# Third gating cycle of a Trainium2 transformer block: regrouped, second layer in three passes, gates finished on ScalarE

## What is computed

```python
def _twist(x):
    o_r, o_i, p_r, p_i = jnp.split(x, 4, axis=-1)
    return jnp.concatenate([p_r, -p_i, -o_r, o_i], axis=-1)
...
gf = _global_net(x.mean(axis=1, keepdims=True), ...)
out = x
for _ in range(NUM_CYCLES):                    # 3
    tf = _coupling_net(out, ...)               # 512 -> 512 -> 256 -> 128 -> 1, gelu, sigmoid
    combined = 0.7 * gf + 0.3 * tf
    coupling = BASE_COUPLING + adaptive_range * (combined - 0.5) * 2.0
    out = out + coupling * _twist(out)
return out
```

## Time and profile before

| | us |
|---|---|
| median of 3 runs | 1733.85 |
| lowest and highest | 1733.26, 1734.9 |
| the profiled execution | 1734.33 |
| its span, first to last instruction | 1732.5 |
| feed-forward part within the span | from about 1243.4 to the end |

### The profile page before, as it was taken

The page is one execution under the profiler, slowest core; times in us unless marked ns, Lnnn a source line. Parts: engine busy times, 40 slices in busy tenths (PEclk is TensorE's granted clock), DMA queues, the critical chain, the costliest instruction groups (busy, mean ns, idle before and its releaser), DMA issues. The chain is left out here.

```text
span 1732.5 us, 34074 instructions
## 1 busy us (share of the span) xinstructions
PE 1703.2 (98%) x12392; PEld 1282.1 (74%) x12392; DVE 1443.0 (83%) x2554; ACT 1237.3 (71%) x2169; POOL 660.4 (38%) x590
## 2 busy tenths in 40 slices
PE   8999999999999999999999999999999999999997
PEld 7888888777777777777777777777775675774873
DVE  6554545999999999999999999999678976968868
ACT  4222224999999999999999999999664374365454
POOL 3432342423278552587432875543235010100100
PEclk9999999999999999999999999999999999999999
DMA  7777675765468665567764676555503514222101
GB/s 279 274 246 284 234 268 153 190 183 135 138 162 191 132 150 123 136 212 142 160 152 118 183 172 134 136 110 152 165 11 93 168 50 122 89 74 49 64 1 49
DMA packets 160951, 254.70 MB, mean 147 GB/s; under 512 B 25488, under 2 KB 77968, under 8 KB 160800
## 3 DMA queue, kind: packets, MB, share of 16 engines
q1 hardware_dynamic: 110416, 158.84, 29.1%
q0 software_dynamic: 49808, 92.82, 23.8%
q10 hardware_dynamic: 576, 1.05, 0.2%
HBM read 168.47 MB, written 84.18 MB: 146 GB/s over the span
## 5 line engine op out<-in xcount | busy, mean ns | idle before, releaser
L1021 DVE CUSTOM_DVE_ANT_0 a_neg<-a_sc_ps,am 128x1024 f32<-128x1024 f32 x512 | 622.0, 1215 | 1.4 <-PE a_sc_ps L853 1.3
L961 ACT ACTIVATE a_prob<-a_neg,a_row_min 128x1024 f32<-128x1024 f32 x512 | 586.2, 1145 | 13.5 <-DVE a_row_min L1021 7.8
L867 PEld LDWEIGHTS a_tr_ps<-ident,a_prob 128*128 128x128 f32 x4096 | 461.2, 140 | 89.3 <-issue 53.4
L867 PE MATMUL a_tr_ps<-ident,a_prob 128*128 128x128 f32 x4096 | 519.8, 274 | 0.9 <-ACT a_probT L939 0.9
L996 DVE COPY a_probT<-a_tr_ps 128x512 f32<-128x512 f32 x512 | 350.7, 685 | 37.4 <-PE a_tr_ps L867 36.0
L939 ACT ACTIVATE a_probT<-a_tr_ps 128x512 f32<-128x512 f32 x512 | 304.4, 595 | 35.4 <-PE a_tr_ps L867 15.9
L749 POOL DMA_DIRECT2D a_q_st<-q_parts x144 | 79.6, 558 | 195.6 <-PE a_sc_ps L853 159.7
L853 PE MATMUL a_sc_ps<-k_first,a_q_st 96*128 96x512 f32 x384 | 126.5, 427 | 0.1
L853 PE MATMUL a_sc_ps<-a_k_st,a_q_st 96*128 96x512 f32 x384 | 126.2, 427 | 0.0
L887 PE MATMUL a_o_ps<-a_probT,a_v 128*32 128x256 f32 x2048 | 123.6, 382 | 0.6 <-ACT a_o L950 0.6
L887 PE MATMUL a_o_ps<-a_probT,v_first 128*32 128x256 f32 x2048 | 123.8, 382 | 0.0
(11 more groups left out here) (223 smaller groups left out, 3140.8 us busy)
## 6 DMA issues: line engine op xcount, KB each, us to landing
a_q_st<-q_parts POOLq DMA_DIRECT2D x144, 128.0 KB, 3.8
k_first<-k_parts POOLq DMA_DIRECT2D x24, 512.0 KB, 7.9
a_k_st<-k_parts POOLq DMA_DIRECT2D x24, 512.0 KB, 8.3
a_m_raw<-mask SPq DMA_DIRECT2D x24, 512.0 KB, 5.2
a_adj_raw<-adj SPq DMA_DIRECT2D x24, 512.0 KB, 6.2
k_parts<-p_out_hi SPq DMA_DIRECT2D x32, 256.0 KB, 4.4
k_parts<-p_out_lo SPq DMA_DIRECT2D x32, 256.0 KB, 6.6
v_all<-p_v_out SPq DMA_DIRECT2D x8, 1024.0 KB, 4.4
```

Source lines behind the costliest of these rows:

```text
L867: last = pe.transpose(tr_ps[:, bank(u, half), j * P:(j + 1) * P], prob[:, r % NPROB, t * P:(t + 1) * P], ident[:])
L961: act.activation(prob[:, r % NPROB, :], neg[:, r % 2, :], ACT.Exp, scale=-1.0, bias=row_min[:, r % 2:r % 2 + 1], accum_out=row_sum[:, r // ...
L1021: dve.tensor_tensor_reduce(out=neg[:, r % 2, :], in0=sc_ps[:, r % 2, :], in1=am[:, 2 * qb + qt, :], scale=-1.0, scalar=3.4e38, op0=ALU.add ...
```

## The change

`SPLIT` becomes the pair of cycles (0, 2): the second layer of the first and the third cycle is done in three passes. As w2_hi and w2_lo are overwritten by the next attention tile before the third cycle, POOL copies them (`keep_w2`) to the place of pair_hi and pair_lo, which are free after the first layer. In batch 0 this stands ahead of POOL's last `split_weighted`. Gelu tiles of the second cycle, and the rounded ones of the third, lie where the second half's attention tiles X1 are; so that half's load is now released by the last second layer of the batch, and comes behind the first half's.

The third cycle is regrouped: u = (beta B + A) + c1 (B - beta A), with beta = c0 and the value in brackets kept from the second cycle. VectorE computes B - beta A (`turned`) while the second gate is still being computed, in pieces placed between the mixes, and then scales and adds (`third_cycle`). ScalarE does the affine step of the gate that VectorE did (`gate`: tanh, then an Identity with scale and bias). The rows that SP carries are beta and c1, and VectorE forms the two coefficients from the columns (`gated_columns`). On ScalarE most gelus of the next cycle's tiles now stand ahead of the gate. Two result tiles of the first half have their twisted part made by ScalarE.

```diff
@@ -1045,7 +1045,7 @@
     CYCLES = 3
-    SPLIT = 1
+    SPLIT = (0, 2)
...
@@ -1072,8 +1072,11 @@
         w2_lo = nc.alloc_sbuf_tensor_at("f_w2_lo", [P, ET, F2], F32R, offset=SB_K0 + 12288)
+        w2_kept = [nc.alloc_sbuf_tensor_at(f"f_w2_kept{part}", [P, ET, F2], F32R, offset=sb.offset + 4096 * part) for part in range(2)]
         pair_hi = sb("f_pair_hi", [P, 2, CH], F32R)
         pair_lo = sb("f_pair_lo", [P, 2, CH], F32R)
+        h1_second = [nc.alloc_sbuf_tensor_at(f"f_h1_second{j}", [P, ET, CH], F32, offset=SB_AM + 8192 * j) for j in range(NJ)]
+        u_hi_third = [nc.alloc_sbuf_tensor_at(f"f_u_hi_third{j}", [P, ET, CH], F32R, offset=SB_AM + 8192 * j) for j in range(NJ)]
...
@@ -1255,12 +1255,18 @@
         def _(pool):
+            def keep_w2(b):
+                pool.wait_ge(product_ready, 4 * ET * NJ * (b + 1))
+                pool.wait_ge(w2_lo_ready, b + 1)
+                for kept, tile in zip(w2_kept, (w2_hi, w2_lo)):
+                    pool.dma_start(kept[:], tile[:]).then_inc(w2_kept_loaded, 16)
             def load_attention(b, j, part):
                 if j == 0:
-                    pool.wait_ge(z2_ready, 2 * turn(b - 1, SPLIT - 1, 1) + 2)
+                    pool.wait_ge(z2_ready, 2 * turn(b - 1, 0, 1) + 2)
+                    pool.wait_ge(w2_kept_loaded, 32 * b)
                 else:
-                    pool.wait_ge(product_ready, 4 * ET * (NJ * (b - 1) + j + 1))
+                    pool.wait_ge(z2_ready, 2 * turn(b - 1, CYCLES - 1, 1) + 2)
...
@@ -1292,10 +1298,13 @@
                 if first:
-                    for n in range(LATE, 2 * B * GPB):
+                    for n in range(LATE, 2 * B * GPB - 1):
                         split_weighted(pool, weighted, n)
+                keep_w2(b)
+                if first:
+                    split_weighted(pool, weighted, 2 * B * GPB - 1)
                 if more:
-                    for j in (1, 0):
+                    for j in range(NJ):
...
@@ -1373,20 +1382,24 @@
                         pe.wait_ge(shared_read, 4 * ET * NJ * (b + 1))
+                if n in SPLIT:
+                    pe.wait_ge(w2_lo_ready, b + 1)
+                    if n:
+                        pe.wait_ge(w2_kept_loaded, 32 * (b + 1))
+                w_hi, w_lo = w2_kept if n else (w2_hi, w2_lo)
+                high = u_hi_third[j] if n else u_hi[j]
                 for t in tiles:
...
+                    if n in SPLIT:
                         pe.wait_ge(u_lo_ready, ET * turn_split(b, n, j) + t + 1)
...
+                    else:
+                        pe.wait_ge(h1_ready, ET * k + t + 1)
+                    for m in range(2):
+                        ms = slice(m * P, (m + 1) * P)
+                        if n in SPLIT:
+                            last = three_pass(pe, acc[:, 2 * j + m, :], w_hi[:, t, ms], w_lo[:, t, ms], high[:, t, :], u_lo[j][:, t, :],
                                               t == 0, t == ET - 1)
...
+                        else:
+                            last = pe.matmul(acc[:, 2 * j + m, :], w2[:, t, ms], h1_second[j][:, t, :], start=t == 0, stop=t == ET - 1)
...
@@ -1511,9 +1524,15 @@
                 k = ((CYCLES - 1) * b + n - 1) * NJ + j
+                if n == 1:
+                    act.wait_ge(product_ready, 4 * ET * NJ * (b + 1))
+                elif m == 0:
+                    act.wait_ge(z2_ready, 2 * turn(b, 1, j) + 2)
                 act.wait_ge(u_ready, ET * k + m + 1)
-                if n < SPLIT:
-                    act.activation(u_hi[j][:, m, :], u[j][:, m, :], ACT.Gelu, bias=small.b1[:, m:m + 1])
+                if n == 1:
+                    act.activation(h1_second[j][:, m, :], u[j][:, m, :], ACT.Gelu, bias=small.b1[:, m:m + 1]).then_inc(h1_ready, 1)
+                    return
+                act.activation(u_hi_third[j][:, m, :], u[j][:, m, :], ACT.Gelu, bias=small.b1[:, m:m + 1])
...
@@ -1527,7 +1546,12 @@
                 act.wait_ge(z4_ready, turn(b, n, j) + 1)
-                act.activation(coef[:, j, :], z4[:, j, :], ACT.Tanh, scale=0.5, bias=small.half_b4[:]).then_inc(t_ready, 1)
+                if n == 0:
+                    wait(act, rows_stored, 32 * NJ * b)
+                act.activation(coef[:, j, :], z4[:, j, :], ACT.Tanh, scale=0.5, bias=small.half_b4[:]).then_inc(tanh_ready, 1)
+                act.wait_ge(base_ready, b + 1)
+                act.wait_ge(tanh_ready, NJ * ((CYCLES - 1) * b + n) + j + 1)
+                act.activation((beta if n == 0 else coef)[:, j, :], coef[:, j, :], ACT.Identity, scale=small.range_3[:], bias=base[:]).then_inc(t_ready, 1)
...
@@ -1581,23 +1605,36 @@
                     other = (b, (k - 1) // NJ + 1, (k - 1) % NJ)
+                    def next_h1(*tiles):
+                        if between:
+                            for m in tiles:
+                                h1(*other, m)
+                    if k == 3:
+                        next_h1(0)
                     h2_half(b, n, j, 0)
                     h2_half(b, n, j, 1)
                     if k == 0:
                         act.wait_ge(gz3_ready, b + 1)
                         act.activation(g_tanh[:], z4[:, 1, 3:4], ACT.Tanh, scale=0.5, bias=small.half_gb3[:]).then_inc(g3_ready, 1)
-                    if between:
-                        h1(*other, 0)
+                    if k == 5:
+                        twist(b, 0, 2)
+                    next_h1(1 if k == 3 else 0)
                     h3_all(b, n, j)
-                    if between:
-                        h1(*other, 1)
+                    if k == 5:
+                        twist(b, 0, 3)
+                    if k < 3:
+                        next_h1(1, 2)
+                        gate(b, n, j)
+                        next_h1(3)
+                        continue
+                    if k == 4:
+                        next_h1(1)
+                    next_h1(2, 3)
                     if n < CYCLES - 1:
                         gate(b, n, j)
                     else:
                         gate_columns(b, j)
-                    if between:
-                        h1(*other, 2)
-                        h1(*other, 3)
...
@@ -1664,58 +1701,71 @@
                 dve.tensor_tensor(w2_lo[:], w2[:], w2_hi[:].bitcast(F32), ALU.subtract).then_inc(w2_lo_ready, 1)
...
+            def split_u(b, n, j, tiles=range(ET)):
+                for m in tiles:
                     dve.wait_ge(h1_ready, ET * turn(b, n, j) + m + 1)
...
+                    dve.tensor_tensor(u_lo[j][:, m, :], u[j][:, m, :], (u_hi_third if n else u_hi)[j][:, m, :].bitcast(F32), ALU.subtract).then_inc(u_lo_ready, 1)
+            def in_turn(first, second):
+                first(0)
+                for m in range(1, ET):
+                    first(m)
+                    second(m - 1)
+                second(ET - 1)
+            def second_cycle(b, j):
+                k = ET * (NJ * b + j)
+                dve.wait_ge(t_ready, turn(b, 0, j) + 1)
+                def scale(m):
+                    dve.tensor_tensor(u[j][:, m, :], Bt[j][:, m, :], beta[:, j, :], ALU.mult).then_inc(mul_ready, 1)
                 def add(m):
                     dve.wait_ge(mul_ready, k + m + 1)
...
+                    dve.tensor_tensor(u[j][:, m, :], u[j][:, m, :], A[j][:, m, :], ALU.add).then_inc(u_ready, 1)
+                in_turn(scale, add)
+            def turned(b, j, tiles):
+                k = ET * (NJ * b + j)
+                dve.wait_ge(u_ready, ET * ((CYCLES - 1) * b * NJ + j + 1))
+                for m in tiles:
+                    dve.tensor_tensor(A[j][:, m, :], A[j][:, m, :], beta[:, j, :], ALU.mult).then_inc(twist_step, 1)
+                    if m > tiles[0]:
+                        subtract(j, m - 1, k)
+                subtract(j, tiles[-1], k)
+            def subtract(j, m, k):
+                dve.wait_ge(twist_step, k + m + 1)
+                dve.tensor_tensor(Bt[j][:, m, :], Bt[j][:, m, :], A[j][:, m, :], ALU.subtract).then_inc(turned_ready, 1)
+            def third_cycle(b, j):
+                k = ET * (NJ * b + j)
+                dve.wait_ge(t_ready, turn(b, 1, j) + 1)
+                dve.wait_ge(turned_ready, k + ET)
+                def scale(m):
+                    dve.tensor_tensor(Bt[j][:, m, :], Bt[j][:, m, :], coef[:, j, :], ALU.mult).then_inc(B_scaled, 1)
+                def add(m):
+                    dve.wait_ge(B_scaled, k + m + 1)
+                    dve.tensor_tensor(u[j][:, m, :], u[j][:, m, :], Bt[j][:, m, :], ALU.add).then_inc(u_ready, 1)
+                in_turn(scale, add)
             def gated_columns(b, j):
                 k = NJ * b + j
+                be, c, al, both = raw_cols[:, j, 0], raw_cols[:, j, 1], cols[:, j, 0], cols[:, j, 1]
                 dve.wait_ge(cols_loaded[j], 32 * (b + 1))
...
+                dve.scalar_tensor_tensor(al, be, -1.0, c, ALU.mult, ALU.mult).then_inc(cols_step, 1)
+                dve.tensor_tensor(both, be, c, ALU.add).then_inc(cols_step, 1)
```

(25 more changed lines are left out.)

83 lines of the change are left out of this document (14 added, 69 removed).

## The result

| | before | after |
|---|---|---|
| median of 7 runs each, us | 1733.9 (1733.26 to 1735.66) | 1739.71 (1739.3 to 1742.27) |
| ratio after / before | | 1.0036, 95% interval 1.0026 to 1.0046 |
| profiled execution / its span, us | 1734.33 / 1732.5 | 1739.71 / 1737.9 |

What follows compares the result with a forecast made beforehand. The prediction took TensorE's own instructions as the bound before, VectorE's order after. Batch 0 with batch 1's start +3.3, two batches -0.3 each, batch 3 +0.8: +3.5 on 1733.85, about 1737.4 us; range 1729 to 1743.

Steps and rivals of the forecast that it cites:

- what would show it: Signs: third-cycle TensorE wait 1 to 2.5 us; batch 0 longer by 2 to 5; batches 1, 2 near 118.4; end about +1.
- Three passes shed 2.3 us a batch: Third cycle's second layer: TensorE sheds 1.17 us a turn, 2.3 a batch, 9.4 in all, if nobody keeps it waiting.
- The order on VectorE is the bound, with 1.75 us of waiting: Third cycle, each batch: TensorE waits 1.75 us for VectorE's first split before turn (2,1)'s three-pass second layer.
- A steady gain of 0.3 us a batch: Each batch after the waiting: layer 3 starts at 1481.4 against 1481.69, a gain of 0.3 us instead of 2.3.
- Batch 0's VectorE row: Batch 0: 20 operations, 12.1 us, plus 4.7 lost to POOL's last split; third cycle may start at 1343.6.
- batch 0 runs 115.1 us ahead of batch 1: From batch 0's third cycle on, batch 1's times less 115.1 us; next batch starts at 1370.0, 4.1 us later.
- Batch 1 gains 0.74 at its start: Start of batch 1: the load that held it shrinks from 6 MB to 4, so 0.74 us goes.
- The end +0.8: End of the kernel: the second half's first row tile starts 0.8 us later, with nothing to hide it in batch 3.
- Covered moves: Copies of w2's parts and the second half's later attention load cost nothing; the load has more than 5 us of cover.
- Rival A: Third cycle's chain is shorter than counted and batch 0's POOL overlap is absorbed: not slower, 1727 us; chance 0.14.
- rival B: Only batch 0's loss of 3.3 us is missing, so no change: 1734 us; chance 0.26.
- rival C: Second half's attention load lands late, costing 2 to 3 us in each of three batches: 1745 us; chance 0.08.

Runs made afterwards that it cites:

- e2: The changed kernel with the third cycle's second layer in plain fp32 again, one gelu per tile and no splits: 1739.03 us, 1.0029 of before.
- e9: The changed kernel with only the first split of the third cycle's second half ahead of that half's last add on VectorE: 1737.28 us, 1.0018 of before.
- e3: The changed kernel with POOL's last split in batch 0 on 2 of 512 columns, leaving that output piece wrong: 1733.76 us, 0.9997 of before.
- e5: The changed kernel with ScalarE's gate ahead of the first half's last third-cycle tile: 1745.40 us, 1.0064 of before.
- e11: e10 with e5's gate order, and VectorE's split of the late tile behind the second half's first two scalings: 1736.13 us, 1.0012 of before.
- e6: e5 with the first split of the third cycle's second half also ahead of that half's last add: 1742.45 us, 1.0047 of before.
- e12: The changed kernel with the copies of the two kept weights behind POOL's last split instead of ahead: 1739.81 us, 1.0027 of before.
- e1: The changed kernel with, on ScalarE, h2's gelus ahead of the first third-cycle tile's in turn (1,1): 1741.68 us, 1.0042 of before.
- e4: The changed kernel with POOL's first late split ahead of the second half's pair splits: 1735.93 us, 1.0010 of before.
- e10: The changed kernel with the second half's first split ahead of its last two adds, e4's edit, and the first half's last output tile finished later: 1732.18 us, 0.9988.
- e7: The changed kernel with the edits of e6 and e4 together: 1738.13 us, 1.0022 of before.

## Why the prediction was right, and where it was off

The direction, the median (1737.4 forecast, 1739.71 measured, range 1729 to 1743) and three of the four signs of "what would show it" came out, with batches 1 and 2 at 118.8 us for "near 118.4"; but batch 0 grew by 6.0 and not by 2 to 5 us. Step by step:

- **Three passes shed 2.3 us a batch**: right. Busy time fell by 2.35 us in batch 1.
- **The order on VectorE is the bound, with 1.75 us of waiting**: right in every term. Within batch 1 (4.35 us later than before from layer 3 of turn (0,0) on) layer 3 of turn (1,1) was forecast at 1462.57 and came at 1467.01 - 4.35 = 1462.66; tile 0 of turn (2,1) at 1474.85, and came at 1474.99. e2 and e9 confirm the cause.
- **A steady gain of 0.3 us a batch**: wrong by 0.36, a size. 0.14 is in the terms up to tile 0, and 0.2 between it and layer 3, 1479.34 to 1486.10, 6.76 us, where I had added 6.55 from single stages.
- **Batch 0's VectorE row**: right. The third cycle was forecast at 1343.6 in before's time, 1342.7 in the change's, which starts 0.9 earlier; it started at 1342.53. The loss to POOL was 4.6 us for a forecast of 4.7, and e3 gives 4.7.
- **From there "batch 0 runs 115.1 us ahead of batch 1"**: this step failed. It carries the shape of batch 1 over to batch 0, and so assumes the same clock. Layer 3 and tile 0 took 1346.47 to 1351.69, 5.2 us instead of 3.2, at the lower level. So the next batch's first projection came 1.8 us later than this step gives.
- **Batch 1 gains 0.74 at its start**: right, 0.72 (its -0.66 with the steady 0.06).
- **The end +0.8**: right, 0.92.
- **The sum**: 3.5 against 6.3 us within the part: 1.9 of the difference is batch 0, 0.7 the steady gain that batches 1 and 2 didn't have, 0.1 batch 3 with the end, and the rest rounding. Between the profiles only 5.4 is left of it, since the part happened to start 0.9 us earlier. That much of the nearness is luck.
- **Covered moves**: right. No wait for the kept weights or for the second half's attention tile; X_lo landed in 7.8 us (median), 9.8 at most.

Rival A fell by the 1.75 us waits, rival B by batch 0, rival C by the absence of any wait ahead of the projections. C had a number wrong: 13.9 us is the slowest landing of an X_hi tile before; an X_lo tile, issued last of the four loads at 1339.35, took 18.5, which by C's own sum would have been some 5 us late. The rule of the Trainium skill (SBUF — State Buffer, section Who interferes with whom), taken over all of POOL's busy time, gave 1740. That is near the result, but for another reason: VectorE's loss was 4.6 us, not 7.07, and the rest was TensorE's clock.

## What to carry to other kernels

Before work is taken from the engine that is always busy, follow the hand-over chain of the stage on the engines that feed it: here one 0.6 us operation taken out of that chain was worth 0.66 us a batch, and 2.35 us less of TensorE's own work was worth nothing. When an instruction is moved, list on every in-order queue what waits for it and what stands behind that (e5, e11). And a wait that a forecast creates on TensorE may have a second price, the clock behind it; in these runs it was paid behind every wait over 4 us, and behind two of about 2.

## What the runs showed of the hardware

**The clock falls in the middle of a kernel.** Behind every wait of 5.24 or 5.25 us (change, e5, e6, e9, e12), and those of 4.63 (e2) and 4.05 (e1), TensorE ran at 1.2 GHz; in the change for 4 us, at a price of 2.0. Of the shorter waits in batch 0, those of 1.75 us (e4, e10, e11), 2.10 (the kernel before) and 2.23 (e5) had no such effect, nor had the 1.75 us of every steady batch of the change, but one of 1.76 us in e7 had, and one of 2.30 in e1. That stretch of e1:

```profile
1316.00:1320.00 4.00, 3.08 (x5) 1.31 (x5) 1.55 (x4) 1.60 (x4) 1.03 (x1) 0.68 0.45 138
```

So a wait's length alone doesn't tell, and a forecast can only give such a wait a second price with a chance. The Trainium skill (TensorE: Matmul & The Clock Gate, Part 1: The HAM clock gate) has it that the clock is halved or not by how busy the array has been of late, and by no level between; the rows above agree, with 0.50 behind the wait and 1.00 elsewhere (0.74, 0.97 and 0.68 are means over stretches in which it changed).

**VectorE can keep POOL out over many operations, but doesn't always.** In the change, e3 and e12 POOL's first operation lasted 3.63, 3.21 (on 2 columns) and 6.59 us. It ended at VectorE's first step of 0.72 us (e3), or about one operation's time behind it (the others; e2, e6 and e9 are the same). That step is where VectorE's difference waits for the product directly before it (`turned`). As I read these rows, that pause let POOL in. After it they took turns: VectorE's operations came up to 1.68 us apart instead of 0.60, POOL's took 1.6 instead of 1.3. This is why moving the copies changed nothing. But the pause is no general condition. In the kernel before, the same POOL operation came in behind a single VectorE operation, with VectorE issuing every 0.60 us, and it was VectorE's next one (1329.84 in the earlier trace rows, 1.75 us) that had to wait:

```profile
1328.62 1.29 DVE L1696 TENSOR_TENSOR f_u<-f_B,f_beta 128x512 f32<-128x512 f32 x2
1329.63 1.41 POOL L132 TENSOR_TENSOR st_o<-st_o,st_rinv 128x512 f32<-128x512 f32 x1 [7.16 <-DMA st_rinv<-rinv_all]
```

What decides between the two cases no run here shows. The Trainium skill (SBUF — State Buffer, section Who interferes with whom) says that whoever issues first holds the pair of SBUF ports that VectorE shares with POOL (GpSimd) for the whole instruction. The row of the kernel before agrees; by the rows of the change, e3 and e12 it was held over a whole run of VectorE's instructions, in the change over four that started after POOL's did (1332.39).
